# Batch 0's first two layer 0 tiles in plain float32, with the weight loads, the operand splits and batch 1's low-rank chain reordered around them

## The chip, the cores and the metric

One core of a Trainium2 chip runs the whole program. The metric is the device time of one execution in microseconds (us), lower being better. The kernel before has a median of 460.23 us over 3 runs (459.65 to 460.66). TensorE (PE, with its weight loads as PEld), VectorE (DVE), ScalarE (ACT) and GpSimd (POOL) run side by side, each in its own program order, and meet only through semaphores. SyncE (SP) issues the DMA transfers.

## The reference

The input x has 8 batches of 256 rows and 1024 features. Four layers follow, each added to its input:

```
x = x + x @ W.T + 0.5 * (x @ lora_A[label]) @ lora_B.T          # layer 0, rank 32, label per batch
x = x + quantised(x)                                            # layer 1
x = x + x @ weight[adapter].T                                   # layer 2, 1024 x 1024 per batch
x = x + (x @ B[adapter].T) @ A[adapter].T                       # layer 3, rank 16
```

Layer 1 counts for each element how many of 8 thresholds its magnitude stays under, picks a step size and a zero point by that count, rounds, clips and scales back; above all thresholds it gives 0. Everything is float32.

## The kernel before, in words

**Tiles.** Features lie on the 128 partitions; a batch is 8 column blocks (k) of 256 rows. A layer 0 weight tile `o` (of 8) holds the 8 blocks of 128 x 128 that give output block `o`. Layer 0's weights are the same for all batches, so they are loaded once and kept split: `w0_hi` is the weight rounded to the short float32r form, `w0_lo` the rest of it. The residual (x itself) comes in by adding an identity to the diagonal block of each weight tile (`add_diag`, L682). x is split in the same way into `x_hi` and `x_lo`. ACT writes the hi part (L457 to L479), DVE subtracts it from the original for the lo part (L691 to L712).

**Layer 0 on PE.** `main0` (L902 to L926) computes a tile as three products of split operands, 3 x 8 = 24 matmuls. `low_rank0` (L940) is x @ lora_A by 8 plain float32 matmuls on narrow weights, four row groups at a time. ACT copies that result out (`drain_low`, L494), `sum_low` on PE adds up the row groups (L955), ACT and DVE split the sum (`low_rank_hi`, L504, `low_rank_lo`, L715), and `close0` (L928) adds the second low-rank product to each output block. `tile0` (L961) sets where these stand among the tiles, which come in the order `ORDER` = 0, 2, 1, 3, 4, 6, 5, 7 (n is the position in this order, so n = 1 is tile 2). After the first four tiles and their closes `l0_done` counts one half of a batch, and ACT copies that half from PSUM into `x2` (`drain_l0`, L510).

**Start.** SP issues the loads in the order of L350 to L369. The raw weight tiles use buffers that layer 1 needs later: tile n lies in half of one of the three candidate buffers (`w0_stage`, L205), and tiles 6 and 7 take the places of tiles 0 and 1, so their loads wait for the splits of those (`load_w0`, L276). For tile 0 and batch 0 of x, loads and splits are cut into halves and quarters. 14 matmuls on the identity (`WARM`, L1075) come before PE's first real work. DVE's hand-written order of the start is L850 to L888, ACT's L656 to L676.

**Layer 1.** The work goes by units: batch 0 is two units of half a batch, batches 1 to 6 one unit each, the last batch three. For each of the 8 levels j, ACT computes a candidate (`candidate`, L556) and from the second level on a mask (`test`, L569), and DVE scales, merges and clips (`scale`, L752, `merge`, L768, `clip`, L760). Between the levels both engines run the other layers' small steps by a list written out by hand (`between`, L579 on ACT and L786 on DVE). In unit 0 that list has the split of batch 1's x at j = 1, the copy of batch 0's second half and batch 1's `drain_low` at j = 3, and `low_rank_hi(1)` at j = 5.

**Layer 2 and PE's order.** PE's program (L1073 on) is fixed: 22 layer 0 tiles first (batches 0, 1 and all but two of batch 2), then for each batch the four quarters of layer 2 (`layer2`, L978, of which L990 is plain float32 on whole operands and L1002 the split product), then seven more layer 0 tiles with layer 3's steps among them. Three waits tie PE to DVE: layer 2 starts when the batch's `x2_done` is counted, its third and fourth quarters wait for DVE's copies of the first and second from PSUM (`drain_l2`, L731), and the first tile of batch b waits until ACT has copied batch b - 1's first half (`x0_done`, L907). For batch 2 that copy waits in its turn for all four `drain_l2` of batch 0:

```
act.wait_ge(l0_done, 2 * b + h + 1)
if b >= SLOTS:
    act.wait_ge(x3_done, 4 * (b - SLOTS) + 4)
act.activation(x2[:, b % SLOTS, h * HW:(h + 1) * HW], l0_ps[:, h, :], ACT.Copy).then_inc(x0_done, 1)
```

## Time and profile before

| | value |
|---|---|
| median of 3 runs | 460.23 us |
| the profiled execution's own time | 459.77 us |
| its span, first to last instruction | 458.0 us |
| PE busy | 446.3 us (97%) |
| PEld busy | 408.1 us (89%) |
| DVE busy | 423.1 us (92%) |
| ACT busy | 357.5 us (78%) |
| DMA, mean over the span | 165 GB/s |

The profile counts an engine as busy from the start of an instruction to its end; overlapping instructions are merged. A plain float32 matmul shows as two MATMUL records, a split one as one. Matmuls overlap one another, so the pace of a group is read from the starts of neighbouring groups and not from the mean duration. An idle time carries the name of what ended it.

### The profile page before, as it was taken

To read this page: it belongs to the slowest core of one execution; us is meant where nothing else is said; L and a number is where in the kernel's file an instruction comes from. 1 tells how busy PE (TensorE), PEld (TensorE's weight loads), DVE (VectorE), ACT (ScalarE), POOL (GpSimd) and SP (SyncE) were. 2 spreads that over 40 slices of the span, in tenths; PEclk is the share of its full clock that TensorE was granted. 3 is DMA by queue.
4 is the path that set the end of the run, shared out by engine and by line. 5 is a ranking of instruction groups with operands and counts; after the bars stand their busy time and mean duration, and the time that the engine had idled before them with its cause. 6 is when DMAs were issued, how large, how long until landed. Compare 5 with 4: busy or idle time off the path is not lost.

```text
span 458.0 us, 7875 instructions
## 1 busy us (share of the span) xinstructions
PE 446.3 (97%) x3118; PEld 408.1 (89%) x3118; DVE 423.1 (92%) x409; ACT 357.5 (78%) x330; POOL 34.6 (8%) x46
## 2 busy tenths in 40 slices
...
GB/s 287 334 241 105 92 135 100 134 224 212 82 167 244 248 89 151 184 220 228 82 180 232 244 92 149 143 215 174 76 188 117 168 63 166 122 212 318 1 92 92
DMA packets 35352, 75.62 MB, mean 165 GB/s; under 512 B 3956, under 2 KB 14068, under 8 KB 34548
## 3 DMA queue, kind: packets, MB, share of 16 engines
...
## 4 chain that ended last, share of the span: by engine, by line
PE 64%; DVE 23%; issue 8%; DMA 2%; ACT 2%; SPq 1%; DVEq 0%; ACTq 0%
PE l_ps L925 31%; PE l_ps L990 18%; DVE quant L784 8%; DVE cand L758 6%; PE l_ps L1002 5%; PE l_ps L1018 3%; DVE cand L766 2%; DVE x L736 2%; PE bx_ps L951 2%; PE bx_ps L1037 2%; DVE quant L778 1%; DMA a_raw<-a 1%; PE l_ps L935 1%; DVE x L835 1%; DMA adapter_ids<-adapters 1%
## 5 line engine op out<-in xcount | busy, mean ns | idle before, releaser
L990 PE MATMUL l_ps<-x,w_sb 128*128 128x256 f32 x672 | 150.3, 380 | 0.9 <-DVE x L736 0.9
L784 DVE COPY_PREDICATED quant<-mask,cand 128x2048 f32<-128x2048 int8 (+2 forms) x77 | 146.0, 1897 | 0.4
L990 PEld LDWEIGHTS l_ps<-x,w_sb 128*128 128x128 f32 x672 | 125.9, 190 | 19.4 <-issue 2.1
L566 ACT ACTIVATE cand<-x,inv_delta 128x2048 f32<-128x2048 f32 (+2 forms) x88 | 134.4, 1527 | 8.8 <-DVE quant L778 7.0
L576 ACT ACTIVATE mask<-magnitude,thr_bias 128x2048 fp8e5<-128x2048 f32 (+2 forms) x77 | 117.5, 1526 | 9.0 <-DVE quant L784 8.2
L758 DVE TENSOR_SCALAR cand<-cand,delta 128x2048 f32<-128x2048 f32 (+2 forms) x88 | 87.6, 996 | 7.7 <-ACT cand L566 7.4
L766 DVE TENSOR_SCALAR cand<-cand,lower,upper 128x2048 f32<-128x2048 f32 (+2 forms) x88 | 92.8, 1055 | 0.4
L925 PE MATMUL l_ps<-x_hi,w_hi 128*128 128x256 f32 x512 | 86.1, 290 | 1.9 <-ACT w_hi L467 1.0
L925 PE MATMUL l_ps<-x_hi,w_lo 128*128 128x256 f32 x512 | 82.8, 283 | 0.0
L925 PE MATMUL l_ps<-x_lo,w_hi 128*128 128x256 f32 x512 | 82.5, 283 | 0.0
L925 PEld LDWEIGHTS l_ps<-x_hi,w_hi 128*128 128x128 f32 x512 | 71.0, 191 | 7.7 <-issue 4.1
L925 PEld LDWEIGHTS l_ps<-x_hi,w_lo 128*128 128x128 f32 x512 | 70.7, 192 | 0.2 <-DVE w_lo L700 0.2
L925 PEld LDWEIGHTS l_ps<-x_lo,w_hi 128*128 128x128 f32 x512 | 70.7, 191 | 0.0
L442 POOL DMA_DIRECT2D w_lo<-w_edge x28 | 26.6, 949 | 238.7 <-ACT w_lo L545 238.7
L514 ACT ACTIVATE x<-l_ps 128x1024 f32<-128x1024 f32 x16 | 16.3, 1019 | 26.7 <-DVE x L736 14.2
L1002 PE MATMUL l_ps<-x_hi,w_hi 128*128 128x256 f32 x112 | 27.7, 328 | 0.0
L736 DVE TENSOR_TENSOR x<-l_ps,x 128x512 f32<-128x512 f32 x32 | 22.2, 696 | 2.0 <-PE l_ps L1018 1.8
L1002 PE MATMUL l_ps<-x_lo,w_hi 128*128 128x256 f32 x112 | 22.5, 282 | 0.0
L1002 PE MATMUL l_ps<-x_hi,w_lo 128*128 128x256 f32 x112 | 22.4, 282 | 0.0
L1002 PEld LDWEIGHTS l_ps<-x_hi,w_hi 128*128 128x128 f32 x112 | 19.3, 190 | 1.5
L536 ACT ACTIVATE bx_split<-bx_ps 128x256 fp32r<-128x256 f32 x8 | 3.1, 381 | 22.2 <-PE bx_ps L1044 14.3
L778 DVE SCALAR_TENSOR_TENSOR quant<-magnitude,sorted_thr,cand 128x2048 f32<-128x2048 f32 (+2 forms) x11 | 19.4, 1764 | 0.0
...
## 6 DMA issues: line engine op xcount, KB each, us to landing
...
```

The source lines that it names most:

```text
L442: pool.dma_start(split_pair(w2_lo, b, q), raw_edges(q), accum_op=ALU.add).then_inc(w2_added[q], 16)
L514: act.activation(x2[:, b % SLOTS, h * HW:(h + 1) * HW], l0_ps[:, h, :], ACT.Copy).then_inc(x0_done, 1)
L566: act.activation(cand[:, c % CANDS, 0:n], x2_unit(u), ACT.Identity, bias=ROUND, scale=inv_delta[:, k:k + 1]).then_inc(rounded, 1)
L576: act.activation(mask[:, m % MASKS, 0:n], magnitude[:, 0:n], ACT.Relu, bias=thr_bias[:, k:k + 1], scale=STEEP, saturate=False).then_inc(ma ...
L736: dve.tensor_tensor(x3[:, cols], l2_bank(b, q), x2[:, b % SLOTS, cols], ALU.add).then_inc(x3_done, 1)
L758: dve.tensor_scalar(t, t, -ROUND, delta[:, k:k + 1], ALU.add, ALU.mult).then_inc(scaled, 1)
L766: dve.tensor_scalar(t, t, lower[:, k:k + 1], upper[:, k:k + 1], ALU.max, ALU.min).then_inc(clipped, 1)
L778: dve.scalar_tensor_tensor(y, magnitude[:, 0:n], sorted_thr[:, G - 1:G], t, ALU.is_gt, ALU.mult)\
L784: dve.copy_predicated(y, mask[:, m % MASKS, 0:n].bitcast(I8), t).then_inc(merged, 1)
L925: nc.tensor.matmul(dst, w[:, o, k * P:(k + 1) * P], v[:, b % 2, k * S:(k + 1) * S], start=(o % 2 == 0 and v is x_hi and w is w0_hi and k = ...
L990: last = nc.tensor.matmul(l2_bank(b, q)[:, i * S:(i + 1) * S], w2_block(b, o, k), x2[:, b % SLOTS, k * S:(k + 1) * S], start=(i == 0 and k ...
L1002: last = nc.tensor.matmul(l2_bank(b, q)[:, i * S:(i + 1) * S], w[:, k * P:(k + 1) * P], v[:, k * S:(k + 1) * S], start=False, stop=(i == 1 ...
```

## The change

PE computes the first two tiles of batch 0 (n = 0 and 1) in plain float32 from the raw weight and raw x as they land (`plain0`, `first_tiles`), block by block; their split forms are still made, for batches 1 to 7. The loads of tiles 0 and 1 are interleaved in halves with the quarters of x. Tiles 6 and 7 load into `quant`, which layer 1 uses for its choice, without a wait. On ACT and DVE the order of the start is new: the split of batch 1's x stands ahead of unit 0 and not in it, tile n = 2 is split in halves, `drain_low(0)` and the low-rank steps come earlier in the order, and DVE's `add_diag(5)` and `add_diag(6)` come behind `split_w0(4)` and `split_w0(5)`. In unit 0, `drain_l0(0, 1)` moves from j = 3 to j = 2 and `low_rank_hi(1)` and `low_rank_lo(1)` from j = 5 to j = 4. The four closes of batches 1 and 2 move behind the fifth tile. The warm-up has 10 matmuls.

```diff
-WARM = 14
+WARM = 10
...
+            if n >= 2 * CANDS:
+                return quant[:, n % 2 * T * P:(n % 2 + 1) * T * P]
...
-            return n + 2
+            return n + 2 if n < 2 else n + 3
...
-                if n >= 2 * CANDS:
-                    sp.wait_ge(w0_split_done, w0_pieces(n - 2 * CANDS))
...
-            sp.dma_start(x_raw[:, 0:CW], x[0, :, 0:CW]).then_inc(x_quarter_loaded, 16)
-            sp.dma_start(w0_stage(0)[:, 0:CW], w0[0, :, 0:CW]).then_inc(w0_half_loaded, 16)
-            sp.dma_start(x_raw[:, CW:HW], x[0, :, CW:HW]).then_inc(x_loaded[0], 16)
-            sp.dma_start(w0_stage(0)[:, CW:2 * CW], w0[0, :, CW:2 * CW]).then_inc(w0_loaded[0], 16)
-            sp.dma_start(x_raw[:, HW:BW], x[0, :, HW:BW]).then_inc(x_loaded[1], 16)
...
+            load_first_x(0, x_quarter_loaded[0])
+            load_first_w0(0, 0, w0_half_loaded[0])
+            load_first_x(1, x_loaded[0])
             sp.dma_start(label_ids[:, :], labels.rearrange("(a n) -> a n", a=1)).then_inc(ids_loaded, 16)
             sp.dma_start(adapter_ids[:, :], adapters.rearrange("(a n) -> a n", a=1)).then_inc(ids_loaded, 16)
-            for n in range(1, 5):
-                load_w0(n)
+            load_first_w0(1, 0, w0_half_loaded[1])
+            load_first_x(2, x_quarter_loaded[1])
+            load_first_w0(0, 1, w0_loaded[0])
+            load_first_x(3, x_loaded[1])
+            load_first_w0(1, 1, w0_loaded[1])
+            load_w0(2)
             sp.wait_ge(ids_loaded, 2 * 16)
             load_a0(0)
+            load_w0(3)
             for q in range(4):
                 sp.dma_start(a3_raw(0)[q * QUAD:(q + 1) * QUAD, :], b0).then_inc(b0_loaded, 16)
+            load_w0(4)
             load_w0(5)
             for dst, src in ((thr, thresholds), (delta, deltas), (zp, zeropoints)):
...
+                if n == 1:
+                    act.wait_ge(w0_loaded[n], 16)
...
-                    act.wait_ge(diag_added, 1)
-                else:
+                act.wait_ge(diag_added, n + 1)
...
-                elif c < 2:
-                    act.wait_ge(w0_split_done, w0_pieces(4 + 2 * c))
+                elif c == 0:
+                    act.wait_ge(w0_split_done, w0_pieces(4))
...
                 s = UNITS[u][0]
                 if u == 0:
-                    if j == 1:
-                        split_batch(1)
+                    if j == 2:
+                        drain_l0(0, 1)
                     if j == 3:
-                        drain_l0(0, 1)
                         drain_low(1)
+                    if j == 4:
+                        low_rank_hi(1)
                     if j == 5:
                         split_x(2, 0)
-                        low_rank_hi(1)
                     if j == 6:
...
-            act.activation(quant[:, 0:1], ident[:, 0:1], ACT.Abs)
-            for h in range(2):
-                split_first_x(h)
-                split_first_w0(h)
+            act.activation(magnitude[:, 0:1], ident[:, 0:1], ACT.Abs)
+            split_first_x(0)
+            split_first_x(1)
+            split_first_w0(0, 0)
             split_first_x(2)
+            split_first_w0(0, 1)
             split_first_x(3)
-            for n in range(1, 5):
-                split_w0(n)
+            split_w0(1)
+            split_first_w0(2, 0)
+            split_first_w0(2, 1)
+            drain_low(0)
+            split_w0(3)
             act.wait_ge(b0_loaded, 4 * 16)
             act.activation(b0_split[:, :], a3_raw(0), ACT.Copy, scale=0.5).then_inc(b0_hi_done, 1)
-            drain_low(0)
-            split_w0(5)
             low_rank_hi(0)
-            split_w0(6)
-            split_w0(7)
+            for n in range(4, T):
+                split_w0(n)
+            split_x(1, 0)
+            split_x(1, 1)
             drain_l0(0, 0)
...
                 s = UNITS[u][0]
                 if u == 0:
-                    if j == 1:
-                        split_x(1, 0)
-                        split_x(1, 1)
-                    if j == 5:
+                    if j == 4:
                         low_rank_lo(1)
                 elif u == 1:
...
                                   mybir.AxisListType.XY, ALU.add, negate=True).then_inc(marks_ready, 1)
             dve.tensor_reduce(fold, ident[:, :].rearrange("p (g r) -> p r g", g=4),
                               mybir.AxisListType.X, ALU.add).then_inc(fold_ready, 1)
+            add_diag(0)
             split_first_x(0)
-            add_diag(0)
-            split_first_w0(0)
+            add_diag(1)
             split_first_x(1)
-            split_first_w0(1)
+            split_first_w0(0, 0)
             split_first_x(2)
-            add_diag(1)
+            split_first_w0(0, 1)
             split_first_x(3)
+            split_w0(1)
             add_diag(2)
-            split_w0(1)
+            split_first_w0(2, 0)
             add_diag(3)
-            split_w0(2)
+            split_first_w0(2, 1)
+            split_w0(3)
             add_diag(4)
-            split_w0(3)
-            split_w0(4)
-            add_diag(5)
             rows = slice(QUAD, 2 * QUAD)
             dve.wait_ge(b0_hi_done, 1)
             dve.scalar_tensor_tensor(b0_split[rows, :], a3_raw(0)[rows, :], 0.5,
                                      b0_split[rows, :].bitcast(F32), ALU.mult, ALU.subtract).then_inc(b0_split_done, 1)
+            low_rank_lo(0)
+            split_w0(4)
+            add_diag(5)
+            split_w0(5)
+            add_diag(6)
             dve.wait_ge(params_loaded, 3 * 16)
             dve.max(sorted_thr[:, :], thr[:, :]).then_inc(param_step, 1)
             dve.reciprocal(inv_delta[:, :], delta[:, :]).then_inc(param_step, 1)
             dve.tensor_scalar(upper[:, :], zp[:, :], -1.0, TOP_LEVEL, ALU.mult, ALU.add).then_inc(param_step, 1)
             dve.scalar_tensor_tensor(lower[:, :], zp[:, :], -1.0, delta[:, :], ALU.mult, ALU.mult)\
                 .then_inc(param_step, 1)
-            add_diag(6)
-            split_w0(5)
+            add_diag(7)
+            split_w0(6)
             dve.wait_ge(param_step, 3)
             dve.tensor_tensor(upper[:, :], upper[:, :], delta[:, :], ALU.mult).then_inc(param_step, 1)
             dve.tensor_scalar(thr_bias[:, :], sorted_thr[:, :], -STEEP, None, ALU.mult).then_inc(param_step, 1)
-            low_rank_lo(0)
-            add_diag(7)
-            split_w0(6)
             split_w0(7)
+            split_x(1, 0)
+            split_x(1, 1)
             dve.wait_ge(param_step, 6)
...
-                for first, end in parts:
-                    if b == 0 and o == 0:
-                        pe.wait_ge(w0_hi_done, 1 if first < HALF else 2)
-                        pe.wait_ge(x_split_done, (first + 2) // 2)
-                    elif b == 0:
+                for first, end in ((0, HALF), (HALF, T)):
+                    if b == 0:
+
+                        pe.wait_ge(x_split_done, 4)
+                        pe.wait_ge(w0_hi_done, w0_pieces(n) - (n == 2 and first == 0))
+                    elif b == 1 and n < 2:
                         pe.wait_ge(w0_hi_done, w0_pieces(n))
-                    elif o == 0 and b < ADDED:
+                    if o == 0 and 0 < b < ADDED:
                         pe.wait_ge(x_split_done, x_pieces(b, first // HALF))
-                    elif o == 0:
+                    elif o == 0 and b >= ADDED:
                         pe.wait_ge(x_added, 16 * (b - ADDED + 1))
                     for w, v in ((w0_hi, x_hi), (w0_hi, x_lo), (w0_lo, x_hi)):
-                        if b == 0 and w is w0_lo:
-                            pe.wait_ge(w0_split_done, w0_pieces(n) if o > 0 or first >= HALF else 1)
+                        if w is w0_lo and b == 0:
+                            pe.wait_ge(w0_split_done, w0_pieces(n) - (n == 2 and first == 0))
+                        elif w is w0_lo and b == 1 and n < 2:
+                            pe.wait_ge(w0_split_done, w0_pieces(n))
                         for k in range(first, end):
 
...
+
+            def plain0(n, k, start=False):
+
+                o = ORDER[n]
+                if k == o:
+                    pe.wait_ge(diag_added, n + 1)
+                nc.tensor.matmul(l0_ps[:, 0, o * S:(o + 1) * S], w0_stage(n)[:, k * P:(k + 1) * P],
+                                 x_raw[:, k * S:(k + 1) * S], start=start, stop=False)
+
+            def first_tiles():
+                pe.wait_ge(x_quarter_loaded[0], 16)
+                pe.wait_ge(w0_half_loaded[0], 16)
+                plain0(0, 1, start=True)
+                plain0(0, 0)
+                pe.wait_ge(x_loaded[0], 16)
+                plain0(0, 2)
+                plain0(0, 3)
+                pe.wait_ge(w0_half_loaded[1], 16)
+                plain0(1, 0, start=True)
+                plain0(1, 1)
+                plain0(1, 3)
+                plain0(1, 2)
+                pe.wait_ge(w0_loaded[0], 16)
+                pe.wait_ge(x_quarter_loaded[1], 16)
+                plain0(0, 4)
+                plain0(0, 5)
+                pe.wait_ge(x_loaded[1], 16)
+                plain0(0, 6)
+                plain0(0, 7)
+                pe.wait_ge(w0_loaded[1], 16)
+                for k in range(HALF, T):
+                    plain0(1, k)
...
                 if i == 0 and 0 < b < 3:
                     low_rank0(b, 0)
-                main0(b, o)
-                if b > 2 or i >= HALF:
+                if n == 0:
+                    first_tiles()
+                elif n > 1:
+                    main0(b, o)
+                if b > 2:
                     close0(b, o)
                 else:
+
                     if b == 0 and i == 1:
                         low_rank0(b, 0)
                     if i == (2 if b == 0 else 1):
                         sum_low(b)
-                    if i == HALF - 1:
+                    if i == (HALF - 1 if b == 0 else HALF):
                         for done in ORDER[:HALF]:
                             close0(b, done)
+                    if i >= HALF:
+                        close0(b, o)
 
             def layer2(b, q):
```

## Rows read from the trace of the kernel before

**Rows 1.** Busy by stretch: us, PE, PEld, DVE, ACT, POOL (records), PEclk, DMA, GB/s

```profile
84.00:110.00 26.00, 26.00 (x160) 23.13 (x158) 25.91 (x20) 23.87 (x20) 3.61 (x3) 1.00 0.86 225
132.00:335.00 203.00, 203.00 (x1429) 185.80 (x1428) 195.13 (x150) 163.08 (x135) 19.08 (x20) 1.00 0.64 173
```

**Rows 2.** Chain of waits that ended last: start us, us, what

```profile
113.07 0.70 DVE x L736
...
113.86 1.04 ACT x L514
...
114.94 3.14 PE l_ps L925 x24
...
129.66 2.88 PE l_ps L925 x24
...
132.66 5.18 PE l_ps L990 x24
...
335.77 1.03 ACT x L514
```

**Rows 3.** PE's timeline: start us, us, line, work, records, idle before

```profile
7.26 0.50 PE L925 MATMUL l_ps<-x_hi,w_hi 128*128 128x256 f32 x2 [1.01 <-ACT w_hi L467]
...
15.50 1.07 PE L951 MATMUL bx_ps<-x_raw,a_raw 128*32 128x256 f32 x16 [0.57 <-DMA a_raw<-a]
...
35.50 1.07 PE L951 MATMUL bx_ps<-x_raw,a_raw 128*32 128x256 f32 x16
```

**Rows 4.** DVE's timeline, the start and unit 0

```profile
11.29 0.29 DVE L689 TENSOR_TENSOR cand<-cand,ident 128x128 f32<-128x128 f32 x1 [0.37 <-DMA cand<-w]
...
14.73 0.29 DVE L689 TENSOR_TENSOR cand<-cand,ident 128x128 f32<-128x128 f32 x1 [0.68 <-DMA cand<-w]
...
18.43 0.29 DVE L689 TENSOR_TENSOR cand<-cand,ident 128x128 f32<-128x128 f32 x1 [1.06 <-DMA cand<-w]
18.76 1.22 DVE L868 SCALAR_TENSOR_TENSOR b_split<-x,b_split 32x1024 fp32r<-32x1024 f32 x1
...
20.74 0.29 DVE L689 TENSOR_TENSOR cand<-cand,ident 128x128 f32<-128x128 f32 x1 [0.36 <-DMA cand<-w]
20.95 1.22 DVE L694 TENSOR_TENSOR w_lo<-cand,w_hi 128x1024 fp32r<-128x1024 f32 x1
22.08 0.16 DVE L879 TENSOR_TENSOR upper<-upper,delta 128x8 f32<-128x8 f32 x1
...
22.35 0.43 DVE L718 TENSOR_TENSOR low_split<-bx_ps,low_split 32x256 fp32r<-32x256 f32 x1
...
26.48 0.75 DVE L758 TENSOR_SCALAR cand<-cand,delta 128x1024 f32<-128x1024 f32 x1 [1.02 <-ACT cand L566]
...
33.55 2.42 DVE L712 TENSOR_TENSOR x_lo<-x_raw,x_hi 128x1024 fp32r<-128x1024 f32 x2
35.83 0.81 DVE L758 TENSOR_SCALAR cand<-cand,delta 128x1024 f32<-128x1024 f32 x1
```

**Rows 5.** ACT's timeline, the start

```profile
17.18 1.06 ACT L665 ACTIVATE b_split<-x 128x1024 fp32r<-128x1024 f32 x1 [1.06 <-DMA x<-b]
...
21.06 1.06 ACT L459 ACTIVATE w_hi<-cand 128x1024 fp32r<-128x1024 f32 x1 [0.57 <-DVE cand L689]
...
24.11 1.01 ACT L514 ACTIVATE x<-l_ps 128x1024 f32<-128x1024 f32 x1
25.19 1.15 ACT L566 ACTIVATE cand<-x,inv_delta 128x1024 f32<-128x1024 f32 x1
```

**Rows 6.** SP's issues, the start

```profile
8.98 0.36 SPq L273 DMA_DIRECT2D a_raw<-a  x1
...
16.68 0.81 SPq L269 DMA_DIRECT2D x_raw<-x  x2
```

**Rows 7.** The warm-up's records (L1075), 3.0 to 4.0 us and 5.0 to 5.5 us

```profile
L1075 PE MATMUL l_ps<-ident x6: 421/421/421, 2.8 to 3.8; 128*128 128x128 f32 x6
...
L1075 PE MATMUL l_ps<-ident x7: 275/275/275, 4.7 to 5.4; 128*128 128x128 f32 x7
```

32 lines of the change are left out of this document (18 added, 14 removed).

## The prediction

> **What bounds the kernel now.** I read the busy time by stretch first. From 132 to 335 us PE is busy for all of 203.00 us and DVE for 195.13; from 84 to 110 us DVE is busy 25.91 of 26.00 us and PE, as the view counts it, all of it [rows 1]. So PE bounds most of the run, and early on the two are level. Next I read the chain of waits, which decides between them. Before 114.9 us it runs through DVE: drain_l2(0, 3) starts at 113.07, ACT's copy of batch 2's first half follows at 113.86, and only then, at 114.94, PE starts batch 3's first tile; from there PE carries the chain until ACT's copy at 335.77 [rows 2]. PE came to that place almost together with the copy (the tile before it ends about 0.3 us earlier by the pace of its matmuls). Call 113.07 to 114.94 the gate. Whatever the start saves on PE alone is lost there; the end moves only as far as DVE's 113.07 moves, and that step waits for no PE result (layer 2's matmuls for it are over by then). Third, the timelines of the start: where PE, DVE and ACT stand when, and which of their waits end with a DMA [rows 3, 4, 5].
>
> **Part 1, the two tiles on PE.** A split tile is 24 matmuls at 2.88 us. 24 records of plain float32 take 5.18 us [rows 2], so a plain tile of 8 matmuls (16 records) is 3.45 us. Two tiles are 6.9 us in place of 5.76: 1.1 us more work, which can start without a split. The split form first started at 7.26 after 1.01 us of waiting for ACT [rows 3]; plain work starts when the first half weight lands and its diagonal is added, about 5.7. I put the end at 12.6 (5.7 + 6.9), if each later piece lands before its turn; the last half comes within the first 2.0 MB. Before, 2.5 MB were down at 11.29 [rows 4], so 2.0 MB are down near 10.0, with 1.7 us of PE work then left. Bounds for the end: 12.4 to 13.6.
>
> low_rank0(0) then needs lora_A. Its DMA was issued at 8.98 [rows 6] and landed at 15.50 less the wake-up, ending a wait of 0.57 on PE [rows 3]. Now the ids are issued two transfers earlier (0.46 us apiece), so the issue is at about 8.0, and only 2.5 MB are queued ahead in place of 3.5. That gives 11.7 at the earliest, 14.5 at the latest (6.5 after the issue as before); I take 12.7. So PE is 15.50 - 12.7 = 2.8 us early (bounds 1.0 and 3.0), and unless ACT and DVE hold up tile n = 2, batch 1 begins at 32.7 and not at 35.50 [rows 3]. The closes of batches 1 and 2 only change places on PE (no work more or less); batch 1's first half is counted a tile, 3 us, later, and ACT asks for it only in unit 1, past 50 us. I cost that at nothing.
>
> **Part 2, how DVE and ACT reach unit 0.** Unit 0's first DVE step stands at 26.48 [rows 4]. Unit 0 then had the lo split of batch 1's x: from 33.55 to the next step at 35.83, 2.28 us [rows 4]. It now lies ahead of unit 0. So the break-even start of unit 0 is 26.48 + 2.28 = 28.76: earlier is a gain at the gate, later a loss, one for one. The DVE idle times at the start (1.06, 0.68, 0.37, 0.36 us for DMAs, 1.02 for ACT [rows 4]) are what the moved split could fill.
>
> The landings. From lora_B's landing at 17.18 [rows 5] to tile 5's at 18.43 [rows 4] is 1.25 us for one tile of 512 KB. The bytes until tile 5 are the same set as before, so tile 5 stays at 18.4. Tile 4, which was ahead of lora_A and lora_B and landed at 14.73 [rows 4], is now behind both: 18.43 - 1.25 = 17.2. lora_B gets one tile ahead: 15.9. Bounds for tile 4: 15.9, where lora_B's slow stretch shares the queue with it, and 18.4, where it shares with tile 5.
>
> The Trainium skill ("DMA: Bandwidth & Descriptors", section "Two DMAs through the same engine are not ordered") says that nothing orders transfers across the 16 engines, so a landing is no simple matter of place in the queue. The trace cannot refute that: I use the order as an estimate, and by that page either end of the tile 4 bounds could come.
>
> The walk from there. ACT has the hi part of tile 3 and of lora_B by 17.0 (lora_B at 15.9 plus 1.06 [rows 5]). DVE adds tile 4's diagonal at 17.2, does lora_B's lo part (18.76 to about 20.0, 1.24 us [rows 4]) to 18.6, and low_rank_lo(0) (22.35 to the next step, about 0.45 us [rows 4]) to 19.0. Its source, sum_low(0), is done near 17.1: PE at 12.7 plus 1.0 for low_rank0, 2.9 for a tile and 0.4. Then comes what the new order costs. Before, add_diag(n + 1) stood ahead of split_w0(n), so ACT could work on the next tile at once. Now add_diag(5) waits behind split_w0(4) and add_diag(6) behind split_w0(5). One round is: diagonal to ACT 20.74 to 21.06, 0.32 us; ACT's hi 1.06 [rows 5]; DVE's lo 1.13 (20.95 to 22.08 [rows 4]); semaphores 0.04; 2.55 us together. DVE is idle for about 1.1 us of it, twice. So ACT starts hi of tile 6 at 19.0 + 2.55 + 1.13 + 0.32 = 23.0, tile 7 at 24.0 (0.95 us a piece), the halves of batch 1's x at 24.9 and 25.9, drain_l0(0, 0) at 26.8; its first candidate starts 1.08 later (24.11 to 25.19) and DVE 1.29 after that (to 26.48) [rows 4, 5]. That is 29.2. By DVE's own work it would be 19.0 + 2 x 2.55 + 1.13 + 0.27 + 1.13 + 2.28 = 28.9, so ACT ends last, by 0.3.
>
> Other inputs are there: batch 1's x was issued at 16.68 [rows 6] behind the same bytes, and landed before 25; low_rank0(0) being earlier cannot make it later. SP passes tiles 6 and 7 without a wait, which changes nothing as these waits had long been over at their issue.
>
> Sum of part 2: 29.2 - 28.76 = +0.4 us. Upper bound for a gain: DVE needs tile 7's lo and batch 1's two halves after the last weight, so no start before 27.0, -1.8. Upper bound for a loss: tile 4 at 18.4 gives +1.6.
>
> **Part 3, unit 0.** ACT too loses about 1.9 us of x splits inside the unit, against DVE's 2.28. The copy at j = 2 and low_rank_hi(1) at j = 4 put 1.0 and 0.3 us on ACT one level earlier; after the two, ACT's candidate is still 0.5 us ahead of DVE by my count (2 x 1.04 us of ACT in a level of 2.63 us of DVE). low_rank_hi(1) needs sum_low(1) on PE: 32.7 + 1.0 + 6.0 + 0.5 = 40.2, and ACT gets there near 40.6. So this part is worth nothing, while its cover is only 0.4 us on PE's side: with PE at its time of before the wait would be 2.3 us, of which 0.9 would reach DVE.
>
> **Part 4, the warm-up.** Four matmuls less. Its records last 421 ns around 3.5 us and 275 ns at 5 us [rows 7]; the granted clock stands at 1.00 throughout, but the pace changes at about 4.3. Twenty records then end near 5.3, before the first plain matmul, so nothing waits for them. Worth nothing either way.
>
> **Sum.** PE 2.8 us early and then 2.8 + 0.3 + 0.4 = 3.5 us idle at the gate; end later by 0.4 us. The profiled execution took 459.77 us (span 458.0, 1.77 around it), so 460.2 for it. It lies 0.46 below the median of the runs, 460.23, and on that median I forecast 460.6.
>
> **The rivals.**
> A, the PE gain gets through (faster). If tile 4 and lora_B land by 16 and the DVE-ACT rounds overlap better than I walked, unit 0 starts between 27.0 and 27.8, and the gate moves by 1.0 to 1.8: 458.4 to 459.2, say 458.8. For it: the idle times in the start that the moved split could fill. Against: the order of add_diag and split_w0, which is in the code. The whole 2.8 (457.4) would need a gate that DVE does not set, against [rows 1, 2].
> B, the start of layer 1 slips (slower). One place: DVE's add_diag(4), waiting for a tile moved behind lora_A and lora_B. Price one for one; it decides from a landing after 17.7, where the end is 0.9 later. At 18.4: 460.23 + 1.6 = 461.8. For it: tile 4 lost its place to about 0.6 MB, part of it slow (before, tiles 3 and 4 together took 3.4 us from 11.29 to 14.73, where two times 1.25 would be 2.5 [rows 4]). Against: the total of bytes is the same.
> C, PE's gap at the gate. The longest idle time of PE after its first matmul in the rows is 1.01 us [rows 3], and the clock stood at 1.00 after it; 3.5 us is new. The granted clock is 1.00 in all rows, so none shows what a longer gap does. If it fell to the lower level at the gate, 2 to 3 us of matmuls at half pace (421 against 275 ns in [rows 7] for the smaller ones) would cost 1.0 to 1.5 us on a PE that is the bound from there: 461.9.
> The Trainium skill ("TensorE: Matmul & The Clock Gate", section "HAM oscillation — how this bites in real kernels") says that idle gaps on PE bring the lower clock back. By that page C could come; no stretch here has a gap long enough to agree or not.
> D, that the change doesn't do what it says: the plain tiles wait for landings and PE gains under 1 us. Then low_rank_hi(1) delays unit 0 by up to 0.9: 461.5.
>
> **Chances.** Forecast (gate moved by -0.7 to +0.9) 0.58; A 0.18; B 0.13; C 0.06; D 0.05. A difference under 0.2%, 0.9 us, cannot be told from none. The forecast lies inside it, A beyond it on the fast side, B, C and D on the slow side: faster 0.18, same 0.58, slower 0.24. The range 458.8 to 461.9 leaves out about one in ten on each side.
>
> **What would show it.** Right: plain tiles on PE from 5.7 to 12.6, low_rank0(0) near 12.7, batch 1 near 32.7; DVE idle about 1.1 us ahead of two lo splits; unit 0's first scale at 29.2; PE idle over 3 us ahead of batch 3's first tile, which starts at 115.3. Wrong: a first scale before 28, or a gate whose last waiter is not DVE's drain_l2; a granted clock under 1.00 after the gate; a DVE step in unit 0 waiting for ACT by over 0.5 us.

## The result, and the profile after

The changed kernel takes 462.08 us (median of 8 runs, 461.31 to 463.23) against 460.00 (459.16 to 460.79) for the kernel before on the same chips: a ratio of 1.0046 [1.0031, 1.0061]. The forecast was 460.6, in a range up to 461.9. It is slower, and by more than the range allowed.

The profiled execution took 462.04 us (span 460.3), against 459.77 (458.0). The chain of waits of the changed kernel (start us, us, what), to hold against [rows 2]:

```profile
27.07 1.90 ACT x_hi L492 x2
28.96 0.91 ACT x L527
...
68.09 0.67 PE bx_ps L1007 x2
...
109.07 0.69 DVE x L754
...
115.26 0.70 DVE x L754
116.04 1.03 ACT x L527
117.12 2.89 PE l_ps L944 x22
...
337.94 1.03 ACT x L527
```

The gate is the same three steps as before: DVE's `drain_l2` (L754 now), ACT's copy, PE's first tile of batch 3. It opens at 115.26 and not at 113.07, 2.19 us later. The copy at 337.94 is 2.17 us later than the one at 335.77 before, so from the gate on nothing else changed: gate to end of span is 345.04 us, before 344.93. By stretch, as in [rows 1], and with the early stretches in which the loads run:

```profile
5.00:8.00 3.00, 3.00 (x14) 2.63 (x14) 1.62 (x4) 1.78 (x3) 0.00 (x0) 1.00 0.85 274
12.00:17.00 5.00, 5.00 (x44) 3.95 (x43) 3.20 (x6) 2.66 (x5) 0.00 (x0) 1.00 1.05 235
...
84.00:110.00 26.00, 26.00 (x159) 23.13 (x158) 25.94 (x19) 24.85 (x21) 2.95 (x3) 1.00 0.84 222
...
132.00:335.00 203.00, 203.00 (x1429) 185.92 (x1428) 195.38 (x147) 165.24 (x137) 19.10 (x20) 1.00 0.63 172
```

The kernel before moved 389 GB/s from 5 to 8 us and 259 from 12 to 17. PE's timeline of the changed kernel, to [rows 3] and [rows 7]:

```profile
1.53 4.64 PE L1130 MATMUL l_ps<-ident 128*128 128x128 f32 x20 [1.53 <-POOL ident L433]
6.03 7.43 PE L952 MATMUL l_ps<-x_raw,cand 128*128 128x256 f32 x32
13.38 1.07 PE L1000 MATMUL bx_ps<-x_raw,a_raw 128*32 128x256 f32 x16
...
33.74 1.07 PE L1000 MATMUL bx_ps<-x_raw,a_raw 128*32 128x256 f32 x16
...
68.09 0.67 PE L1007 MATMUL bx_ps<-parts,low_sum 128*128 128x256 f32 x2 [1.61 <-ACT parts L515]
...
117.12 0.74 PE L944 MATMUL l_ps<-x_hi,w_hi 128*128 128x256 f32 x4 [2.06 <-ACT x L527]
```

The plain tiles run from 6.03 without a wait, `low_rank0(0)` starts 2.1 us earlier and batch 1 1.76 us earlier. All of it is idle time again by the gate: 1.61 us at 68.09, where PE waits for ACT's `drain_low(2)`, and 2.06 us at 117.12. DVE's timeline of the changed kernel, to [rows 4]:

```profile
19.01 0.29 DVE L706 TENSOR_TENSOR cand<-cand,ident 128x128 f32<-128x128 f32 x1 [0.96 <-DMA cand<-w]
19.34 1.22 DVE L882 SCALAR_TENSOR_TENSOR b_split<-x,b_split 32x1024 fp32r<-32x1024 f32 x1
20.58 0.43 DVE L736 TENSOR_TENSOR low_split<-bx_ps,low_split 32x256 fp32r<-32x256 f32 x1
21.05 1.22 DVE L711 TENSOR_TENSOR w_lo<-cand,w_hi 128x1024 fp32r<-128x1024 f32 x1
...
23.60 1.23 DVE L711 TENSOR_TENSOR w_lo<-cand,w_hi 128x1024 fp32r<-128x1024 f32 x1 [1.13 <-ACT w_hi L473]
...
26.16 1.23 DVE L711 TENSOR_TENSOR w_lo<-quant,w_hi 128x1024 fp32r<-128x1024 f32 x1 [0.64 <-ACT w_hi L473]
...
28.59 2.35 DVE L730 TENSOR_TENSOR x_lo<-x_raw,x_hi 128x1024 fp32r<-128x1024 f32 x2
31.25 0.76 DVE L776 TENSOR_SCALAR cand<-cand,delta 128x1024 f32<-128x1024 f32 x1 [0.31 <-ACT cand L579]
```

DVE waits for tile 4 until 19.01 (17.2 was forecast), then twice for ACT by the exchange of `add_diag` and `split_w0`, and unit 0's first scale is at 31.25 (29.2 forecast; 26.48 before). ACT and SP, to [rows 5] and [rows 6]:

```profile
17.98 1.06 ACT L682 ACTIVATE b_split<-x 128x1024 fp32r<-128x1024 f32 x1 [1.19 <-DMA x<-b]
...
22.51 1.06 ACT L473 ACTIVATE w_hi<-cand 128x1024 fp32r<-128x1024 f32 x1 [2.11 <-DVE cand L706]
```

```profile
6.55 0.36 SPq L275 DMA_DIRECT2D a_raw<-a  x1
...
9.68 0.91 SPq L279 DMA_DIRECT2D cand<-w  x2
...
14.57 0.81 SPq L271 DMA_DIRECT2D x_raw<-x  x2
```

Two numbers carry the rest. "First scale" is the start of unit 0's first `scale` on DVE, "gate" the start of `drain_l2(0, 3)`, both in the profiled execution. From the first scale to the gate it is 84.01 us in the changed kernel and 86.59 before: the x split moved out of unit 0 is worth 2.58. So a first scale at 26.48 + 2.58 = 29.06 is break-even. Each profile is one execution, and the same start does not always come out the same: experiment 11 has the start of before and its gate at 113.87 for 113.07, experiment 5 has the start of the changed kernel and its gate at 113.92 for 115.26. And the eight runs of the changed kernel fall in two groups: granted clock 0.997 or more over the run, 461.31 to 462.11 us; 0.994, 462.63 to 463.23.

### The profile page after: what moved, and what is told of

It reads as the page before. It is cut to its first block, busy times and chain, and to the rows that moved or that the text cites. A ratio compares the mean times of both kernels' runs of the same rounds, so it can differ in the third digit from the quotient of the medians.

```text
span 460.3 us, 7843 instructions
## 1 busy us (share of the span) xinstructions
PE 447.1 (97%) x3094; PEld 408.3 (89%) x3094; DVE 423.6 (92%) x410; ACT 357.4 (78%) x331; POOL 33.6 (7%) x46
## 4 chain that ended last, share of the span: by engine, by line
PE 61%; DVE 17%; issue 8%; ACT 7%; DVEq 0%; ACTq 0%
PE l_ps L944 23%; PE l_ps L1045 23%; PE l_ps L1057 6%; DVE quant L802 6%; DVE cand L776 5%; ACT cand L579 3%; PE l_ps L1073 3%; PE bx_ps L1092 1%; DVE x L754 1%; DVE cand L784 1%; DVE quant L796 1%; ACT mask L589 1%; PE bx_ps L1000 1%; ACT x L527 1%; PE l_ps L986 1%
## 5 line engine op out<-in xcount | busy, mean ns | idle before, releaser
L1045 PEld LDWEIGHTS l_ps<-x,w_sb 128*128 128x128 f32 x672 | 126.1, 190 | 19.2 <-issue 2.1
L776 DVE TENSOR_SCALAR cand<-cand,delta 128x2048 f32<-128x2048 f32 (+2 forms) x88 | 87.3, 992 | 6.7 <-ACT cand L579 6.5
L944 PE MATMUL l_ps<-x_hi,w_hi 128*128 128x256 f32 x496 | 82.9, 290 | 2.1 <-ACT x L527 2.1
L944 PE MATMUL l_ps<-x_hi,w_lo 128*128 128x256 f32 x496 | 79.8, 283 | 0.0
L944 PE MATMUL l_ps<-x_lo,w_hi 128*128 128x256 f32 x496 | 79.7, 283 | 0.0
L944 PEld LDWEIGHTS l_ps<-x_hi,w_hi 128*128 128x128 f32 x496 | 68.7, 191 | 7.3 <-issue 3.7
L944 PEld LDWEIGHTS l_ps<-x_hi,w_lo 128*128 128x128 f32 x496 | 68.4, 192 | 0.0
L944 PEld LDWEIGHTS l_ps<-x_lo,w_hi 128*128 128x128 f32 x496 | 68.3, 192 | 0.0
L454 POOL DMA_DIRECT2D w_lo<-w_edge x28 | 25.5, 912 | 239.5 <-ACT w_lo L558 239.5
L1057 PE MATMUL l_ps<-x_hi,w_hi 128*128 128x256 f32 x112 | 27.7, 329 | 0.0
L754 DVE TENSOR_TENSOR x<-l_ps,x 128x512 f32<-128x512 f32 x32 | 21.9, 688 | 2.0 <-PE l_ps L1073 1.8
L1057 PE MATMUL l_ps<-x_lo,w_hi 128*128 128x256 f32 x112 | 22.5, 283 | 0.0
L1057 PE MATMUL l_ps<-x_hi,w_lo 128*128 128x256 f32 x112 | 22.5, 282 | 0.0
L1057 PEld LDWEIGHTS l_ps<-x_hi,w_hi 128*128 128x128 f32 x112 | 19.3, 190 | 1.4
```

The costliest lines, as they stand in the source:

```text
L454: pool.dma_start(split_pair(w2_lo, b, q), raw_edges(q), accum_op=ALU.add).then_inc(w2_added[q], 16)
L754: dve.tensor_tensor(x3[:, cols], l2_bank(b, q), x2[:, b % SLOTS, cols], ALU.add).then_inc(x3_done, 1)
L776: dve.tensor_scalar(t, t, -ROUND, delta[:, k:k + 1], ALU.add, ALU.mult).then_inc(scaled, 1)
L944: nc.tensor.matmul(dst, w[:, o, k * P:(k + 1) * P], v[:, b % 2, k * S:(k + 1) * S], start=(o % 2 == 0 and v is x_hi and w is w0_hi and k = ...
L1045: last = nc.tensor.matmul(l2_bank(b, q)[:, i * S:(i + 1) * S], w2_block(b, o, k), x2[:, b % SLOTS, k * S:(k + 1) * S], start=(i == 0 and k ...
L1057: last = nc.tensor.matmul(l2_bank(b, q)[:, i * S:(i + 1) * S], w[:, k * P:(k + 1) * P], v[:, k * S:(k + 1) * S], start=False, stop=(i == 1 ...
```

## The experiments

All medians stand beside the kernel before on the same chip.

**1. Only PE's two tiles back to split form.**

```diff
-                if n == 0:
-                    first_tiles()
-                elif n > 1:
-                    main0(b, o)
+                main0(b, o)
```

> The changed kernel with tiles n = 0 and 1 of batch 0 computed from the split operands again, as before, and all else (loads, ACT's and DVE's order, closes, warm-up) as changed. Theory (the end hangs on when DVE starts unit 0, and that on the landing of tile 4 and the rounds after it; PE only waits at the gate): PE reaches low_rank0(0) 1 to 2.5 us later, DVE's first scale stays at 31.2 (at most 0.3 later, since low_rank_hi(0) comes later), the gate at 115.3 and the time within 0.4 us of the changed kernel's, 462.1. Rival (the two plain tiles cost PE their 1.1 to 1.7 us of extra work, and the end moves with it): 460.4 to 461.0.

467.92 us against 459.66, 1.0174 [1.0161, 1.0188]. All theories missed it. PE's timeline, its windows (columns as in [rows 1]), and DVE's timeline:

```profile
11.56 1.22 PE L944 MATMUL l_ps<-x_hi,w_hi 128*128 128x256 f32 x4 [5.39 <-DVE x_lo L724]
...
19.56 1.07 PE L1000 MATMUL bx_ps<-x_raw,a_raw 128*32 128x256 f32 x16
```

```profile
8.00:12.00 4.00, 0.44 (x2) 0.44 (x3) 2.82 (x6) 2.94 (x4) 0.00 (x0) 0.68 1.04 384
12.00:16.00 4.00, 4.00 (x21) 4.00 (x21) 2.86 (x5) 1.15 (x2) 0.00 (x0) 0.50 1.04 227
```

```profile
22.07 1.23 DVE L711 TENSOR_TENSOR w_lo<-cand,w_hi 128x1024 fp32r<-128x1024 f32 x1 [5.92 <-ACT w_hi L473]
...
35.74 0.75 DVE L776 TENSOR_SCALAR cand<-cand,delta 128x1024 f32<-128x1024 f32 x1 [0.32 <-ACT cand L579]
```

PE idles 5.39 us, its granted clock falls to 0.50 (the 1.2 GHz level) and groups of four take 0.85 us and not 0.48. `low_rank0(0)` is 6.2 us late, ACT stands in front of `drain_low(0)` for 6.1 us, and hi of tile 3, which the new order puts behind it, holds up DVE. Part of this belongs to the edit: the changed kernel's `main0` lets batch 0 begin only when all four quarters of x are split (`pe.wait_ge(x_split_done, 4)`), where the kernel before began tile 0 quarter by quarter, at 7.26. So the run shows that the new order on ACT and DVE can't bear a late PE; it does not price the plain tiles alone. The clock fell at the gate as well (gate to end 346.4 us).

**2. The diagonals ahead again**, `add_diag(n + 1)` before `split_w0(n)`.

```diff
-            split_w0(4)
             add_diag(5)
-            split_w0(5)
+            split_w0(4)
             add_diag(6)
+            split_w0(5)
```

> The changed kernel with add_diag(5) ahead of split_w0(4) and add_diag(6) ahead of split_w0(5) on DVE, as in the kernel before. Theory: the DVE idle times of 1.13 and 0.64 us ahead of two lo splits and ACT's of 2.11 and 1.50 shrink; the first scale comes 1.3 to 1.8 us earlier, at 29.4 to 29.9 in place of 31.25, the gate moves by as much, and the time is 460.3 to 460.8, half to one us above the kernel before. Rival (the start of unit 0 is set by the weights' landings alone, so the order on DVE is free): no change, 462.1.

461.53 against 459.66, 1.0032 [1.0020, 1.0044]. First scale 29.82, gate 113.82, both as expected, though 0.76 of the 1.43 us is tile 4, which DVE took up at 18.25 and not 19.01 from the same loads. The time is not as expected: from gate to end 346.4 us, not 345.0. Its window at the gate, and PE there:

```profile
115.00:120.00 5.00, 4.32 (x23) 4.32 (x24) 4.97 (x4) 4.83 (x6) 0.88 (x1) 0.66 0.30 52
```

```profile
115.68 1.22 PE L944 MATMUL l_ps<-x_hi,w_hi 128*128 128x256 f32 x4 [2.05 <-ACT x L527]
```

After a gap of 2.05 us the granted clock fell to 0.66 as a mean over these 5 us, and the first four matmuls took 1.22 us, as in experiment 1, and not 0.74. That is rival C, and it costs 1.4.

**3. The x split back in unit 0**, the rest as changed.

```diff
-            split_x(1, 0)
-            split_x(1, 1)
...
+                    if j == 1:
+                        split_x(1, 0)
+                        split_x(1, 1)
```

> The changed kernel with the split of batch 1's x back in unit 0 at j = 1 on ACT and DVE. Theory (the moved split is worth one for one what unit 0 loses by it): the first scale is at 29.3 (1.9 us of ACT's splits less ahead of it), unit 0 is 2.3 us longer, and the gate and the time end 0 to 0.5 us later than in the changed kernel: 462.1 to 462.6. Rival (the split ahead of unit 0 is what delays layer 1): 460.0 to 460.4.

464.75 against 459.66, 1.0099 [1.0080, 1.0118]; missed. First scale 28.99, but unit 0 grew by 4.8 us (88.80 to the gate, not 84.0). Of the 4.8, about 2.3 is the split's own work on DVE. Then PE had to wait 2.62 us for the split, which stands at 36.05 here, and the clock fell behind that gap too; `sum_low(1)` came at 44.73 and not 40.65, and ACT waited 2.81 us for it:

```profile
37.43 0.71 PE L945 MATMUL l_ps<-x_hi,w_hi 128*128 128x256 f32 x4 [2.62 <-DVE x_lo L730]
```

```profile
37.00:42.00 5.00, 4.57 (x26) 4.60 (x27) 5.00 (x7) 4.78 (x6) 0.00 (x0) 0.66 0.47 137
```

```profile
45.36 0.38 ACT L521 ACTIVATE low_split<-bx_ps 128x256 fp32r<-128x256 f32 x1 [2.81 <-PE bx_ps L1008]
```

In the kernel before the split inside unit 0 held nobody up: it was done at 35.8 and PE came to it at 36.50. Here unit 0 starts 2.5 us later, PE comes 1.8 us earlier, and ACT asks for `sum_low(1)` one level earlier. How much each of the three does was not run apart. The clock fell once more at the gate (0.66 from 120 to 125 us).

**4. The first loads in the order of before** (second half of x whole, tile 1 whole, the ids behind x; PE, ACT and DVE take these first pieces in the same order), the rest as changed.

```diff
+            load_first_w0(0, 1, w0_loaded[0])
+            sp.dma_start(x_raw[:, HW:BW], x[0, :, HW:BW]).then_inc(x_loaded[1], 16)
...
-            load_first_w0(1, 0, w0_half_loaded[1])
...
+            load_w0(1)
```

> The changed kernel with the first 2.5 MB loaded in the pieces and the order of the kernel before (second half of x whole, tile 1 whole, the ids behind x), PE computing tile 0 whole and then tile 1, still plain; lora_A, tile 3, lora_B, tiles 4 to 7 as changed. Theory (part of tile 4's lateness comes from the pieces and the ids in the first 5 us): tile n = 2 lands near 11.3 and not 12.4, tile 4 1.0 to 1.3 us earlier than 19.0, the first scale 0.5 to 1.2 us earlier, and the time 461.0 to 461.6. Rival (only the place of tile 4 behind lora_A and lora_B counts): tile 4 at 18.7 to 19.2 again and 462.1.

461.98 against 459.66, 1.0052 [1.0032, 1.0072]. First scale 30.42, gate 114.38, 0.9 earlier than changed. Its window:

```profile
5.00:8.00 3.00, 2.42 (x13) 1.63 (x11) 1.52 (x4) 1.92 (x4) 0.00 (x0) 1.00 1.00 372
```

The rate is 372 GB/s where the halves had 274. It is no chance reading: in the nine profiles with the halves it is 274 to 319, in the nine with the first loads as before 361 to 396. So the halves do cost, as expected, though 0.9 us alone is no more than the landings spread from run to run. The clock fell in this profile as well (0.72 from 115 to 120 us), and in half of the runs (462.6 to 463.6 at 0.994 to 0.996, 461.0 to 461.4 at 0.997 or more); that hides the gain in the median, which is above the 461.0 to 461.6 expected.

**5. PE's gap filled** by seven more matmuls whose results are overwritten.

```diff
+                    if n == 3 * T:
+                        for _i in range(FILL):
+                            nc.tensor.matmul(l3_ps[:, 0:P], ident[:, :], ident[:, :], start=True, stop=True)
```

> The changed kernel with 7 extra matmuls on the identity (128 columns, plain, into a PSUM bank that is free there) on PE ahead of batch 3's first tile, where PE waits 2.06 us at the gate; their results are not used. Theory of the clock (PE's gap at the gate lets the granted clock fall after it in a part of the executions, and that adds 1 to 1.5 us to those; the extra work fills about 1.6 us of the gap): gate at 115.3 as in the changed kernel, granted clock 0.998 or more in all runs, all times between 461.2 and 461.9. Rival (the gap has no effect; the spread of the changed kernel is of another origin): median 462.1 and single runs up to 463 with a mean clock of 0.994, or later by what the extra matmuls cost.

461.06 against 459.69, 1.0033 [1.0020, 1.0045]. The gap is 0.58 us, no run is under 0.997, and gate to end is 345.0. The loss left is 1.37 us, so the clock's share of the 2.08 is 0.7 in the median. The changed kernel's own five runs at 0.997 or more have a median of 461.66, 1.66 above 460.00, which would leave the clock 0.4. Tile 4 was taken up at 17.56 here, from the same loads, so the gate came at 113.92 and not at 115.3 as expected.

**6. Tile 4 loaded ahead of lora_B.**

```diff
+            load_w0(4)
             for q in range(4):
                 sp.dma_start(a3_raw(0)[q * QUAD:(q + 1) * QUAD, :], b0).then_inc(b0_loaded, 16)
-            load_w0(4)
```

> The changed kernel with the load of tile 4 ahead of lora_B's, everything else as changed. Theory (ahead of split_w0(4) stand both tile 4's landing and lora_B's: landing, ACT's hi 1.06, DVE's lo 1.24, low_rank_lo 0.47): tile 4 lands by 17, lora_B at 18.7 to 19.2 in place of 17.9, DVE's lo of tile 4 starts at 21.4 to 22.0 (21.05 as changed), the first scale at 31.6 to 32.2 and the gate 0.3 to 0.9 later: 462.2 to 463.2. Rival (the start of unit 0 follows tile 4's landing one for one, as case B of the prediction had it): first scale at 29.0 to 29.8 and 460.2 to 461.0.

464.31 against 459.69, 1.0086 [1.0072, 1.0100]. Slower, not faster:

```profile
20.34 1.22 DVE L882 SCALAR_TENSOR_TENSOR b_split<-x,b_split 32x1024 fp32r<-32x1024 f32 x1 [2.75 <-ACT b_split L682]
```

lora_B lands at 19.2, its lo part stands ahead of tile 4's on DVE, and the first scale is at 32.25, the gate at 116.38. The start waits for the later of the two, in either order. The clock fell in four of the five runs, the profiled one among them (gate to end 346.3 us), and with it the median lies 1.1 above the range expected.

**7. Experiments 2, 4 and 5 together**, with tile 1's split behind `add_diag(2)` and ACT's `drain_low(0)` behind tile 3.

```diff
-            drain_low(0)
             split_w0(3)
+            drain_low(0)
```

> The changed kernel with the first 2.5 MB loaded as before, add_diag(2), (5) and (6) each ahead of the split that they stood behind, ACT's hi part of tile 3 ahead of drain_low(0), and the 7 extra matmuls at the gate. Theory (DVE's idle time ahead of the gate is what counts, and the costs found are additive: 1.4 us for the diagonals, 0.9 for the first loads, 1.5 for the clock): first scale at 28.2 to 29.0, gate at 112.2 to 113.0, granted clock 1.0, 458.9 to 459.8: level with the kernel before or up to 0.2% faster. Rival (the loads cap it, so the parts overlap): first scale at 29.5 or later, gate at 113.6 or later, 460.1 or more.

460.92 against 459.69, 1.0026 [1.0016, 1.0035]. First scale 30.00, not 28.2 to 29.0: the loads cap it. DVE's timeline:

```profile
17.16 0.29 DVE L706 TENSOR_TENSOR cand<-cand,ident 128x128 f32<-128x128 f32 x1 [0.85 <-DMA cand<-w]
...
21.58 0.29 DVE L706 TENSOR_TENSOR quant<-quant,ident 128x128 f32<-128x128 f32 x1 [0.47 <-DMA quant<-w]
...
24.06 0.29 DVE L706 TENSOR_TENSOR quant<-quant,ident 128x128 f32<-128x128 f32 x1 [0.77 <-DMA quant<-w]
```

**8. The plain tiles alone, on the kernel before.**

```diff
+                if n == 0:
+                    first_tiles()
+                elif n > 1:
+                    if n == 2:
+                        pe.wait_ge(x_split_done, 4)
+                    main0(b, o)
```

> The kernel before with one part of the change alone: batch 0's first two tiles in plain float32, on the loads and orders of before (tile 0 whole, then tile 1; the loads of tiles 6 and 7 also wait until PE has read the two raw tiles). Theory (PE's time at the start is worth nothing while lora_A lands at 15.4 and DVE sets the gate): low_rank0(0) at 15.4 to 15.6, batch 1 at 35.4 to 35.6, gate at 113.0 to 113.2, and the time within 0.3 us of the kernel before. Rival (plain tiles cost PE 1.1 us that reach the end): 0.8 to 1.3 us slower. Second rival (they free PE, and the end moves): 0.5 us or more faster.

459.75 against 459.69, 1.0004 [0.9992, 1.0015]. `low_rank0(0)` at 15.94 waits 1.27 us for lora_A, batch 1 starts at 35.77, and PE waits 0.46 us at the gate. Nothing gained, nothing lost.

**9 and 10. lora_B by one transfer that reads the 32 rows four times**, on the kernel before, and on kernel 7.

```diff
-            for q in range(4):
-                sp.dma_start(a3_raw(0)[q * QUAD:(q + 1) * QUAD, :], b0).then_inc(b0_loaded, 16)
+            sp.dma_start(a3_raw(0), b0.unsqueeze(0).to_broadcast([4, R0, D])).then_inc(b0_loaded, 16)
```

> The kernel before with lora_B's four copies (each to 32 partitions) loaded by one transfer to all 128 partitions in place of four. Theory (the stretch from 12 to 17 us in which the DMA engines are busy but move only 220 GB/s comes from lora_B's transfers, and the landings of all later weight tiles hang on it): lora_B lands 0.5 to 2 us earlier, tiles 5 to 7 as well, the first scale 0 to 1 us earlier, the gate by as much less its slack of 0.3 us on PE: 459.2 to 459.8, against 459.7 of the kernel before. Rival (the same bytes cost the same however they are issued): landings and time unchanged.

> The combined kernel of the run before (first loads as before, the diagonals ahead, tile 3's hi part ahead of drain_low(0), 7 extra matmuls at the gate) with lora_B loaded by one transfer. Theory (DVE and ACT wait there for the landings of tiles 4, 6 and 7 at 17.2, 21.6 and 24.1, and the gate follows the first scale by 84.0 us in every kernel that has the moved split): those landings 0.5 to 2 us earlier, first scale at 28.3 to 29.5, gate at 112.3 to 113.5 and the end 345 us after the gate: 459.1 to 460.3. Rival (landings unchanged by it): first scale at 30.0, 460.9.

467.39 against 459.89, 1.0162 [1.0148, 1.0175], and 468.00, 1.0179 [1.0160, 1.0199]. Both missed, the same way: ACT's timeline and the window of experiment 9. lora_B is there at 24.8, for 17.2 with four transfers.

```profile
24.82 1.06 ACT L664 ACTIVATE b_split<-x 128x1024 fp32r<-128x1024 f32 x1 [8.23 <-DMA x<-b]
```

```profile
16.00:20.00 4.00, 4.00 (x40) 3.29 (x39) 1.85 (x2) 0.60 (x1) 0.00 (x0) 1.00 1.05 188
```

**11. A gap at the gate in the kernel before.** 16 matmuls (two products) of batch 2's last tile are left out.

```diff
-                    for w, v in ((w0_hi, x_hi), (w0_hi, x_lo), (w0_lo, x_hi)):
+                    for w, v in ((w0_hi, x_hi), (w0_hi, x_lo), (w0_lo, x_hi))[:1 if b == 2 and n == T - 1 else 3]:
```

> The kernel before with 16 of the 24 matmuls of batch 2's last layer 0 tile left out (its lo products, so that part of the output is less exact), which stands right ahead of the gate: PE has 1.9 us less work and waits there about 2.2 us in place of 0.3; DVE's gate is untouched at 113.1. Theory of the clock (a gap of 2 us on PE at this place is enough for the granted clock to fall behind it, whatever kernel has it): in half or more of the runs a stretch below 1.00 follows the gate, and those runs take 1.2 to 1.6 us more: 461.0 to 461.4, with the others at 459.7. Rival (what drops the clock belongs to the changed start, not to the gap): 459.7 in all runs and a granted clock of 1.00 behind the gate.

461.09 against 459.89, 1.0030 [1.0014, 1.0046], with less work on PE. Six runs at a granted clock of 0.994 to 0.996 took 461.5 to 463.5, six at 0.997 or more 459.3 to 460.7. The gap alone does it, in half of the executions; the profiled one, with a gap of 2.07 us, held 1.00.

**12. Experiments 2 and 5 together.**

> The changed kernel with the two diagonals ahead and the 7 extra matmuls at the gate. Theory (the costs are additive: the start of unit 0 and the clock): first scale at 29.4 to 30.2, gate 84.0 later, end 345.0 after the gate, 460.1 to 460.9, no run with a clock under 0.997; 0.6 to 1.4 us below the same kernel without the extra matmuls (461.53). Rival (the clock falls elsewhere once the gate is filled): 461.3 or more.

459.98 against 459.89, 1.0006 [0.9997, 1.0015]: the two are additive and the loss is gone. Against experiment 5 the diagonals alone bring 1.3 us in the median (0.09 above the kernel before, not 1.37). First scale 28.78, 0.6 earlier than expected, gate 112.95, PE's gap 0.51:

```profile
115.00:120.00 5.00, 5.00 (x49) 4.28 (x49) 4.96 (x3) 4.34 (x6) 1.50 (x2) 1.00 0.32 55
```

**13 and 14. lora_B laid out four times in memory, one transfer of 128 different rows**, on the kernel before, and on the changed one.

```diff
-            for q in range(4):
-                sp.dma_start(a3_raw(0)[q * QUAD:(q + 1) * QUAD, :], b0).then_inc(b0_loaded, 16)
+            sp.dma_start(a3_raw(0), b0).then_inc(b0_loaded, 16)
...
-        "b0": np.asarray(L0_cond_lora_B_w).T,
+        "b0": np.concatenate([np.asarray(L0_cond_lora_B_w).T] * 4, axis=0),
```

> The kernel before with lora_B laid out four times over in memory, and loaded by one transfer of 128 rows of 4 KB at addresses of their own (the same 512 KB into the same place). Theory (the repeated reads of the same rows are what halves the DMA rate from 12 to 16 us): no stretch under 300 GB/s there but for lora_A's, lora_B 1.0 to 2.0 us earlier than 17.1, the first scale up to 1.5 us earlier; but PE had only 0.3 us to wait at the gate and then sets the pace, so 459.3 to 459.8 against 459.8 of the kernel before. Rival (the engines are slow there because of lora_A or the 32-byte packets): landings and rate unchanged, first scale at 26.5.

> The changed kernel with lora_B laid out four times over in memory and loaded by one transfer. Theory: tile 4 lands at 16.3 to 17.3 in place of 17.6 to 19.0, the first scale at 28.6 to 29.6, the gate 84.0 later, the end 345.0 after the gate where the clock holds and 346.4 where it falls behind PE's gap: median 460.2 to 461.2, single runs from 459.6 to 461.9. Rival (the lateness is from the halves and the ids in the first loads): tile 4 at 17.6 or later and 461 to 462.

On the kernel before: 459.15 against 459.58, 0.9989 [0.9980, 0.9998], the fastest version here, by 0.1%. First scale 25.65, gate 112.66; PE starts batch 3 at 114.53, without a wait. On the changed kernel: 461.85, 1.0045 [1.0033, 1.0057]. The windows of experiment 14:

```profile
12.00:16.00 4.00, 4.00 (x36) 2.98 (x35) 2.75 (x6) 2.64 (x5) 0.00 (x0) 1.00 1.03 409
16.00:20.00 4.00, 4.00 (x34) 3.94 (x33) 3.61 (x5) 2.12 (x3) 0.00 (x0) 1.00 0.65 226
115.00:120.00 5.00, 4.68 (x26) 4.55 (x26) 4.97 (x4) 4.46 (x6) 1.00 (x2) 0.66 0.31 54
```

```profile
66.38 0.67 PE L1006 MATMUL bx_ps<-parts,low_sum 128*128 128x256 f32 x2 [0.56 <-ACT parts L514]
...
115.31 0.75 PE L943 MATMUL l_ps<-x_hi,w_hi 128*128 128x256 f32 x4 [1.98 <-ACT x L526]
```

The changed kernel and experiments 2, 3, 5 and 12, with the same loads but for lora_B, moved 202 to 255 GB/s from 12 to 16 us; with one transfer of 128 rows it is 409, and DVE no longer waits for tile 4. The edit changes three things at once: the rows differ, there is one transfer and not four, and it fills 128 partitions where each of the four fills 32. Experiment 9 is no clean test of the first, since its one transfer has another shape again (4 copies of 32 rows). So which of them frees the rate is not shown. First scale 29.54, gate 113.45 (1.8 earlier than changed), and still a gap of 1.98 us on PE. The median, above the 460.2 to 461.2 expected, stays up by the clock: nine of eleven runs are at 0.996 or less, and the two shortest, at 0.997 and 0.998, took 459.8 and 460.7.

**15 and 16. The same on kernel 12 and on kernel 7.**

> The changed kernel with the two diagonals ahead, the 7 extra matmuls at the gate and lora_B laid out four times over. Theory (start of unit 0 and gate as one): first scale at 27.6 to 28.4, gate at 111.6 to 112.4, PE's wait there under 0.6 us, end 345.0 after the gate: 458.4 to 459.2, 0.1 to 0.3% faster than the kernel before. Rival (another landing takes over: tiles 6, 7 or batch 1's x cap the start): first scale at 28.7 or later and 459.5 or more.

> The combined kernel (first loads as before, diagonals ahead, tile 3's hi part ahead of drain_low(0), 7 extra matmuls) with lora_B laid out four times over. Theory: first scale at 27.6 to 28.6 in place of 30.0, 458.4 to 459.4. Rival (PE's plain tiles, late here because they take the landings of the first loads as before, or ACT's chain after tile 7's landing cap it): first scale at 29 or later, 460 or more.

460.25, 1.0013 [1.0004, 1.0021], and 460.63, 1.0023 [1.0014, 1.0032]. First scale 29.28 and 29.45; both missed. The next landing is late instead, tile 6's, while the loads run at 207 GB/s from 16 to 20 us (experiment 15; the DMA engines are busy for 0.57 of that time):

```profile
21.75 0.29 DVE L707 TENSOR_TENSOR quant<-quant,ident 128x128 f32<-128x128 f32 x1 [0.81 <-DMA quant<-w]
```

## Why the prediction was wrong

**What bounds the kernel: right.** The gate sets the end. In all profiles with the clock held behind the gate, gate to end is 344.9 to 345.1 us, and PE's 1.76 us of head start at batch 1 reached the end nowhere. Rival A is out.

**Part 1: right in kind, 0.7 us off in size.** The plain tiles ended near 13.4 (12.6 forecast, bounds to 13.6) and `low_rank0(0)` was 2.1 us early, inside the bounds of 1.0 to 3.0. lora_A was issued at 6.55 and not at 8.0, and PE did not wait for it. Experiment 8 shows the head start needs the earlier lora_A. What I did not see: the new order on ACT and DVE needs an early PE (experiment 1).

**Part 2: the step that failed.** "18.43 - 1.25 = 17.2" for tile 4. It landed at 19.0, outside my bound of 18.4; lora_B at 17.9, where I had 15.9. From there the walk held: lo of tile 4 at 21.05 for 19.0, and from it to the first scale 31.25 - 21.05 = 10.20 for 29.2 - 19.0 = 10.2, with the two waits of about 1.1 us (measured 1.13, and 0.64 with the parameter steps filling the rest). The error of the first scale, 2.05, is the landing's 1.8 and 0.25 of DVE steps behind it. Two things in it were wrong. I took the bytes until tile 5 to be down at 18.4 as before, but with the first loads cut into halves the stretch from 5 to 8 us moved 274 GB/s and not 389 (372 with that undone, experiment 4; in experiment 7, which undoes it too, DVE took tile 4 up at 17.16, the time forecast). And I priced "lora_B's slow stretch" at its bytes, while lora_B's four transfers, as they are, about halve the rate for whatever is queued with them (experiment 14 against 2 and 3). With the same loads DVE took tile 4 up at 17.56, 18.22, 18.25, 18.65 and 19.01 in five profiles: always later than 17.2, three times inside my bound. The Trainium skill ("DMA: Bandwidth & Descriptors", "Two DMAs through the same engine are not ordered") says that nothing orders transfers across the 16 DMA engines. The runs bear on that only by this spread of 1.45 us, which a fixed place in the queue does not explain. Experiment 6 corrects rival B, too: not tile 4 alone but the later of tile 4 and lora_B sets the start.

**Part 3: right.** The inner moves cost nothing, and first scale to gate got 2.58 shorter where 2.28 was forecast. The break-even start is 29.06 and not 28.76. The sum then is 31.25 - 29.06 = 2.19, what the gate moved by; rival B's price of one for one is confirmed in ten kernels with the changed unit 0 (first scale to gate 83.9 to 84.2, at starts from 28.78 to 35.74); experiments 16 and 10 are exceptions, with 84.7 and 85.8. The kernels with unit 0 as before took 86.6 to 87.3 (experiments 8, 9, 11 and 13), so 2.58 is the low end of what the moved split brings.

**Part 4: 0.8 us off, without effect.** The 20 records took 4.64 us, so the warm-up ended near 6.1 and not 5.3. The plain tiles follow at once; their first half weight was there at 5.91, when DVE took it up, so at most 0.1 us was lost.

**The gap: smaller than forecast, and dearer.** 2.06 us for 3.5, and it does not follow the gate. PE first waited 1.61 us at 68.09 for ACT's `drain_low(2)`, a wait I had not looked for. From that step to PE's first tile of batch 3 it is 48.9 to 49.1 us in every kernel with the changed unit 0, and 47.0 before, where PE did not wait at either place. What PE is early by beyond that is waited out at 68 us. So the gap is 1.98 to 2.11 us wherever the gate stands, from 113.45 (experiment 14) to 119.72 (experiment 1). Rival C had 6 in 100, since no row of before held such a gap. The profile of experiment 2 shows its price (346.4 - 345.0 = 1.4 us), experiment 11 shows that the gap alone is enough, experiments 5 and 12 show it gone with the gap. I had priced it at 1.0 to 1.5 us, from 2 to 3 us of matmuls at half pace; no row gave me that stretch, so the size was in part luck. It comes in 3 of the 8 executions of the changed kernel, 6 of 12 in experiment 11 and 9 of 11 in experiment 14, so the median carries a part of it, 0.4 to 0.7. The Trainium skill ("TensorE: Matmul & The Clock Gate", "HAM oscillation — how this bites in real kernels") says that idle gaps on PE bring the lower clock back. The runs agree where the clock fell; behind the same gap it held in the others.

In the median, 1.37 us of the 2.08 is the late start (experiment 5: 461.06 - 459.69), the other 0.7 the clock; by the changed kernel's own runs it is 1.66 and 0.4. Either way the late start alone would have stayed inside the range, and so would the clock alone. Rivals B and C were each priced at 461.8 to 461.9 and given a chance as if they excluded each other, but nothing makes them do so: the gap is there however late the gate is, and they came together.

**What stays open.** Why the same loads land up to 1.5 us apart; what in lora_B's four transfers is slow, the repeated rows or the 32 partitions of each; why the rate drops to 207 to 255 GB/s from 16 to 20 us in experiments 4, 7, 14, 15 and 16, which hides what the diagonals would bring there (it is not lora_B alone, since 4 and 7 load it in four transfers, and the DMA engines were busy for only 0.56 to 0.73 of that time); why a gap of 2 us drops the clock in one execution and not in the next.
